# The mask of a cross attention, added on TensorE by tiles of 64 by 64 in place of 32 by 32

## The reference

```python
q = split_heads(hidden_states @ Wq, q_len)
k = split_heads(hidden_states @ Wk, q_len)
v = split_heads(hidden_states @ Wv, q_len)
q = q * cos + _rotate_half(q) * sin
k = k * cos + _rotate_half(k) * sin
scores = jnp.einsum('bhqd,bhkd->bhqk', q, k) * inv_sqrt_d
scores = scores + attention_mask
w = jax.nn.softmax(scores.astype(jnp.float32), axis=-1)
attn_output = jnp.einsum('bhqk,bhkd->bhqd', w, v)
...
a_scores = jnp.tanh(gate) * jax.nn.softmax(a_scores, axis=-1)
attn_output = attn_output + jnp.einsum('bhqk,bhkd->bhqd', a_scores, a_v)
return attn_output @ Wo
```

## Time and profile before

| What | Value |
|---|---|
| median of 3 runs | 3669.77 us (3666.87 to 3670.79) |
| the profiled execution | 3669.14 us |
| its span, from the first to the last instruction | 3667.4 us |
| TensorE busy over the span | 3012.6 us (82%) |
| DVE, ACT busy over the span | 2337.3 us (64%), 1624.9 us (44%) |
| mean granted TensorE clock | 0.919 of full speed |
| the stage of the change | about 143 to 725 us of the span |

### The profile page before, as it was taken

The page is one execution under the profiler, slowest core; times in us unless marked ns, Lnnn a source line. Parts: engine busy times, 40 slices in busy tenths (PEclk is TensorE's granted clock), DMA queues, the critical chain, the costliest instruction groups (busy, mean ns, idle before and its releaser), DMA issues. The chain is left out here.

```text
span 3667.4 us, 76638 instructions
## 1 busy us (share of the span) xinstructions
PE 3012.6 (82%) x28335; PEld 2124.4 (58%) x28336; DVE 2337.3 (64%) x6171; ACT 1624.9 (44%) x4064; POOL 372.6 (10%) x461
## 2 busy tenths in 40 slices
PE   7899999934378799999999999658776889976998
PEld 6566666511156466666666566436554777764786
DVE  6654555488868576676676666677677128846663
ACT  2244444457634455555555555313365224422341
POOL 2100000000033011111111111000011000000110
PEclk9899999955589799999999999879899999989899
DMA  3000000000040000000000000200000000000803
GB/s 101 24 24 23 17 24 15 2 0 0 9 147 12 4 2 1 3 1 1 3 1 1 3 1 2 87 14 0 8 11 6 0 1 1 0 28 26 224 33 108
DMA packets 94866, 88.76 MB, mean 24 GB/s; under 512 B 17440, under 2 KB 83680, under 8 KB 94176
## 3 DMA queue, kind: packets, MB, share of 16 engines
q1 hardware_dynamic: 88496, 77.74, 7.1%
q10 hardware_dynamic: 5808, 7.41, 0.6%
q0 software_dynamic: 384, 1.05, 0.1%
HBM read 77.79 MB, written 8.39 MB: 23 GB/s over the span
## 5 line engine op out<-in xcount | busy, mean ns | idle before, releaser
L3170 PE MATMUL bank<-L1w_w,L1x_xqT 128*128 128x512 f32 x640 | 304.5, 599 | 2.1 <-DVE L1x_xqT L3438 2.1
L3444 DVE TENSOR_REDUCE L1x_ssq<-L1x_square 128x4 f32<-128x512 f32 x192 | 131.5, 685 | 185.6 <-ACT L1x_square L3297 179.7
L1048 DVE TENSOR_REDUCE L0x_top<-bank 128x4 f32<-128x512 f32 x256 | 159.1, 684 | 103.2 <-PE bank L974 100.1
L1033 ACT ACTIVATE L0x_P<-bank,L0x_level 128x512 f32<-128x512 f32 x256 | 155.1, 688 | 156.6 <-PE bank L994 156.6
L3396 POOL TENSOR_TENSOR L1x_square<-L1x_square,L1x_total 128x512 f32<-128x512 f32 x128 | 133.1, 1040 | 604.2 <-DVE L1x_total L3472 604.2
L890 DVE TENSOR_TENSOR x_sb<-x_sb,bank 128x256 f32 (+1 forms) x112 | 47.0, 419 | 231.3 <-PE bank L208 188.0
L3321 ACT ACTIVATE L1x_square<-bank,L1x_top 128x128 f32<-128x128 f32 x512 | 182.0, 375 | 19.7 <-DVE L1x_top L3466 19.7
L3231 PE MATMUL bank<-L1w_wp,L1x_catb 128*128 128x256 bf16 x1536 | 188.4, 273 | 0.1
L3297 ACT ACTIVATE L1x_square<-bank 128x512 f32<-128x512 f32 x192 | 114.8, 598 | 146.8 <-PE bank L3170 146.8
L3170 PEld LDWEIGHTS bank<-L1w_w,L1x_xqT 128*128 128x128 f32 x640 | 115.4, 192 | 99.5 <-issue 95.2
L3327 ACT COPY L1x_PT<-bank 128x512 f32<-128x512 f32 x128 | 76.0, 594 | 216.2 <-PE bank L3214 216.2
(11 more groups left out here) (656 smaller groups left out, 7288.6 us busy)
## 6 DMA issues: line engine op xcount, KB each, us to landing
L0x_mask<-in_maskrows SPq DMA_DIRECT2D x16, 512.0 KB, 3.6
L3f_wgu<-in_L_ffn_Wg SPq DMA_DIRECT2D x8, 704.0 KB, 9.0
L3f_wgu<-in_L_ffn_Wu SPq DMA_DIRECT2D x8, 704.0 KB, 10.4
L1a_wp_quarter<-in_L_xattn_wproj SPq DMA_DIRECT2D x4, 1024.0 KB, 6.2
L3x_ctxT<-in_ctxT SPq DMA_DIRECT2D x32, 128.0 KB, 2.1
L3f_wd<-in_L_ffn_Wd SPq DMA_DIRECT2D x8, 512.0 KB, 8.9
turned_sends<-L3r_sendT ACTq DMA_DIRECT2D x16, 256.0 KB, 2.0
L3e_sends<-turned_sends SPq DMA_DIRECT2D x16, 256.0 KB, 2.9
```

Of the source, the lines that this page charges most:

```text
L1033: act.activation(self.P[:, i % 2, r, :], self.work_bank[r][:, :], ACT.Exp, bias=self.level[:, :]).then_inc(self.p_ready.sem, 1)
L1048: dve.tensor_reduce(self.top[:, s, 16 * c + 4 * r:16 * c + 4 * r + 4], self.work_bank[r][:, :].rearrange("p (h k) -> p h k", h=4), X, ALU.max,
L3170: last = pe.matmul(made_bank[n % 4][:, :], inputs(SOURCE[n], k), w[:, k, 4 * n:4 * n + 4, :], start=(k == 0), stop=(k == C - 1))
L3444: dve.tensor_reduce(ssq[:, 4 * n:4 * n + 4], square[:, (n + 2) % 3, :].rearrange("p (h e) -> p h e", h=4), X, ALU.add).then_inc(sum_ready. ...
```

## The change

`mask_tensor` writes a bank by two matmuls of 64 rows by 64 columns in place of four of 32 by 32. Bank r now takes rows 0 to 63 of the array where r is even and rows 64 to 127 where r is odd; so banks 0 and 2 use the same half of the array's rows, and banks 1 and 3 the other. The mask lies in SBUF as two groups of 64 rows, repeated twice, which makes the tile and its load half as large (256 KB in place of 512 KB). The waits, their order, the scores and all else stay.

```diff
     def mask_tensor(self, pe, mask, r):
         pe.sem_inc(self.masking, 1)
-        rows = self.rows_of(r)
-        for c in range(4):
-            pe.matmul(self.work_bank[r][32 * c:32 * c + 32, :], self.kit.ident[rows, rows],
-                      mask[rows, c, :].unsqueeze(1).to_broadcast([32, 4, 128]), start=True, stop=False,
-                      tile_position=(32 * r, 32 * c))
+        side = slice(64 * (r % 2), 64 * (r % 2) + 64)
+        for c in range(2):
+            pe.matmul(self.work_bank[r][64 * c:64 * c + 64, :], self.kit.ident[side, side],
+                      mask[side, c, :].unsqueeze(1).to_broadcast([64, 4, 128]), start=True, stop=False,
+                      tile_position=(64 * (r % 2), 64 * c))
...
-        mask = ph.sb("mask", [128, SETS, 2, 4, 128])
+        mask = ph.sb("mask", [128, SETS, 2, 2, 128])
...
-    arrays["maskrows"] = in_rows(np.stack([mask, mask.transpose(0, 2, 1)], axis=1))
+    halves = np.stack([mask, mask.transpose(0, 2, 1)], axis=1).reshape(B, 2, 2, 64, S).transpose(0, 3, 1, 2, 4)
+    arrays["maskrows"] = np.ascontiguousarray(np.tile(halves, (1, 2, 1, 1, 1)))
```

## The result

The changed kernel takes 3692.66 us in the median of five runs (3687.03 to 3700.2), against 3670.79 for the kernel before, also in five (3666.87 to 3672.94): 1.006 times, with an interval from 1.0045 to 1.0075. It is slower, as forecast, but by 21.9 us and not by 11, and 2.7 us above the upper end of the range. Its profiled execution took 3692.97 us, 23.8 more than that of before.

The account below looks back on a forecast made before the run. The prediction took TensorE's back-to-back instructions to bound the stage. Its terms, 5.0 + 1.2 + 1.8 + 1.7 + 1.6 = 11.3 us, on the profiled 3669.14 gave 3680.4, stated as 3681 us, with a range of 3673 to 3690.

Parts of the forecast that it names:

- TensorE sets the stage's length and nothing gives a longer set back: Stage from 143 to 725 us: TensorE is 97% busy, so a longer mask set is paid in full.
- Shifts of round 0: 13 steady turns' sets where no bank waits: each grows by 0.38 us, 5.0 us in all (4.4 to 5.6).
- 41 sets with a late bank: Sets whose last bank waits for ACT or DVE: only the wider load adds 0.03 us each, 1.2 us (0 to 2.1).
- Three sets with every bank free: Sets at 143.57 and the stage's last two: grow from 1.27 to 1.87 us, 1.8 us in all (1.7 to 2.0).
- Four others: Sets of the first turn and the end, with one wait or at half clock: 1.6 us more (1.0 to 2.5).
- What comes free: Claim that 16 fewer matmul records a set and half the mask's bytes gain nothing.
- The three sets at the head of the loop's body: First sets behind back edges, instructions late: 0.4 us more, one at half clock about 0.9; 1.7 us (1.2 to 2.5).
- given back: Rival: half-clock spells behind the loop's back edges go and give back 6.8 us; 3673.6 us, no measurable change; chance 0.12.
- banks in single file: Rival: each bank's first pass waits for the previous bank's second; sets take 2.28 us, 23 us more, 3692; chance 0.08.
- Hidden: Rival: later waits swallow the 5.0 us delay of the round 0 shifts, leaving 3675.4 us; chance 0.09.
- no overlap: Rival: array halves don't overlap, 3.6 us a mask set, 96 us more, 3765 us; chance 0.03.
- The rule on strict order: Skill's rule that matmuls start and end strictly in program order; the prediction held the old shape's trace against it.

Follow-up runs that it names:

- run 7: Changed kernel with TensorE's turns written out (no back edge) and round 0 of the shifts kept in 32 by 32: 3658.59 us, 0.9963 of the kernel before.
- run 4: Changed kernel with 64 padding instructions ahead of the loop and 64 behind, 205 left in the packet at the loop's head: 3672.93 us, 0.9997 of the kernel before.
- run 3: Kernel before with 128 padding instructions ahead of the loop and 128 behind, 205 left in the packet at the loop's head: 3666.23 us, 0.9978.
- run 2: Kernel before with 64 padding instructions ahead of the loop and 192 behind, 13 left as in the changed kernel: 3679.91 us, 1.0016.
- run 1: Changed kernel with 192 padding instructions ahead of the loop and 192 behind, 77 left as in the kernel before: 3674.24 us, 1.0007.

## Why the prediction was right or wrong

- *TensorE sets the stage's length and nothing gives a longer set back*: right. The undisturbed turn grew by 0.46 with its sets, and run 7 took 6.8 us off by shortening one set a turn.
- *Shifts of round 0, 1.49 to 1.87, 5.0 us*: right; 1.88 in the trace (0.39 in 13 sets is 5.1).
- *41 sets with a late bank, 0.03 each, 1.2 us*: the mechanism was right, the size about double; against the usual set they grew by some 0.015, 0.6 us. (In the two executions compared their sum fell, by 0.5 us, for the four longer third sets of before.)
- *Three sets with every bank free, 1.8 us*: right; 1.34 to 1.95 in the view of the matmuls, three times 0.61. *Four others, 1.6*: the first grew by 0.2 (1.73 to 1.95) as said; the rest can't be told apart from the edges' and the first turn's own wandering.
- *What comes free: fewer records "cost nothing today, as their issue hides behind the passes"*: this is the blind spot. The issue does hide. But fewer records are also shorter code, and shorter code moves the loop's head.
- *The three sets at the head of the loop's body, 1.7 us*: **the step that failed.** It took the stop behind the back edge as given and asked only what the wider tiles add to it. That much was right in size: 0.4 a set was forecast, and with 205 instructions left the set at the head takes 2.14 to 2.19 up to the next work where the narrow one takes 1.75 (runs 4 and 3). But the stop itself didn't stay: the edges cost 16.7 us more. The bound of 2.5 us was taken from the same picture, so the range couldn't hold the result either. Without this step the forecast's other terms make 9.6 us, and the runs without a second stop show 6.7 and 7.4.
- *The rival "given back"* had the right rows, idle time and half clock behind the edge, and the sentence that TensorE's loop gets shorter by instructions. Its argument that "nothing in the change shortens the idle time at the back edge" held, but the prediction didn't ask what might lengthen it, and something did. Had the head moved the other way, to 205 left, run 4 shows what would have come out: 0.9997, no measurable change.
- *The rival "banks in single file"* gives 3692, the time measured, by accident: it needs sets of 2.28 in round 0, and they take 1.88. "Hidden" and "no overlap" fall by the same rows.
- *The rule on strict order* from the Trainium skill ("TensorE: Matmul & The Clock Gate", Part 3, What overlaps and what doesn't), weighed in the prediction: the new shape's sets of 1.88 leave room for two banks' passes side by side and not for the 2.28 of a single file, so the trace again shows no such order between fp32 passes of different banks.

What stays open: run 2 explains the break in the set but not the whole size. By the intervals the new shape costs 0.2 to 0.7% with 13 instructions left, and 0.1 to 0.2% elsewhere. Part of the difference is seen in the timelines: behind the break at the first edge 12 matmuls take 3.68 where 28 narrow ones take 2.64, 1.04 more, as they run at half clock and one bank behind the other (the whole sets are 1.2 to 1.3 longer at all three); the first stop is longer, 2.86, 3.21 and 2.85 against 2.45, 2.11 and 2.29; and half clock lasted 10.2 us behind all three edges in place of one. Why the clock stays low longer in one kernel than in the other no run here tells. Each reading of a timeline is of one execution.

## What to carry to other kernels

Before costing an edit inside or ahead of a loop at nothing, count what it does to the code: the place of the loop's head in its 16,384-byte packet was worth more here (about 19 us) than the change itself (about 7). A back edge on the engine that sets the time can be looked up in the profile as idle time with "issue" as its releaser, and its second stop, where there is one, began here 1.0 to 2.3 us after the resumption. Padding removed the second stop (runs 1, 3 and 4), and writing the turns out removed both. In this kernel wider tiles cost array time almost only in sets where no bank waits for anything: keep the narrow ones there.

## What the hardware showed

- Behind a back edge TensorE stood idle for 2.1 to 3.2 us wherever its head lay. It stopped a second time if the rest of the packet with the head didn't last until the next packet could be used. That packet started 0.6 to 0.7 us after the resumption (once 1.1), and where TensorE waited for it, it could be used 3.0 to 3.3 us after the resumption. The second stop was 0.7 to 0.95 us with 77 instructions left in the old shape, 2.0 to 2.3 with 13 in either, and none with 77 in the new shape or with 205.
- The clock fell to 0.50 behind all six edges with 13 instructions left (for 6.8 to 10.2 us), behind two of three with 77 in the old shape (6.8), behind none of three with 77 in the new, and behind one of six with 205 (3.4). The first stop alone doesn't decide it: after 2.66 us of idle time run 1 went on at full speed (1.14 for the score matmuls), while in run 3 the one spell stands behind a single stop of 2.44.
- Instructions that compute nothing, 192 ahead of the loop and 192 behind it, shortened a kernel by half a per cent (run 1), by where they put its loop's head.
